# First attention of a two-layer kernel: weight tiles in all four column groups, the sums of four tiles times ones in a step of their own, denominators carried to the query side by DMA

## What is computed

```python
c_q  = h @ W_DQ + b_DQ                 # 32 wide
c_kv = h @ W_DKV + b_DKV               # 32 wide
q = concat(c_q @ W_UQ + b_UQ, c_q @ W_QR + b_QR)        # per head, 128 + 32
k = concat(c_kv @ W_UK + b_UK, h @ W_KR + b_KR)
v = c_kv @ W_UV + b_UV
attn = softmax(q @ k.T / sqrt(160))    # 2048 x 2048 for each of 8 heads
x = x + (attn @ v).reshape(s, 1024) @ W_O + b_O
...
# second attention, 16 heads of 64, 64 anchors
attn = softmax(qk @ W_anchor.T / 8)    # 2048 x 64 for each head
```

## Time and profile before

| what | us |
|---|---|
| median of 3 runs | 790.29 (788.67 to 1489.75) |
| the profiled execution's own time | 788.66 |
| span of its trace | 786.9 |
| 32 blocks of the first attention, first exponential to last | 38.6 to 525.1 |
| second attention, its 16-tile loop, about | 555 to 637 |

### The profile page before, as it was taken

The page is one execution under the profiler, slowest core; times in us unless marked ns, Lnnn a source line. Parts: engine busy times, 40 slices in busy tenths (PEclk is TensorE's granted clock), DMA queues, the critical chain, the costliest instruction groups (busy, mean ns, idle before and its releaser), DMA issues.

```text
span 786.9 us, 12800 instructions
## 1 busy us (share of the span) xinstructions
PE 761.2 (97%) x4302; PEld 473.6 (60%) x4302; DVE 584.4 (74%) x1227; ACT 453.0 (58%) x1035; POOL 569.6 (72%) x485
## 2 busy tenths in 40 slices
PE   8899999999999999999999999999799899999997
PEld 6575555555555555555555555537556589778885
DVE  7878777787777777877777777875887736875564
ACT  4266666656665665666666656564677750455543
POOL 5078999998888788788878878962679771345554
PEclk9999999999999999999999999999999999999999
DMA  6200000000000000000000000003000000000000
GB/s 159 65 3 0 1 2 1 1 2 1 1 1 1 2 1 1 1 1 0 2 1 1 1 1 1 2 1 111 0 1 1 0 2 1 1 1 13 2 14 27
DMA packets 18761, 8.46 MB, mean 11 GB/s; under 512 B 8724, under 2 KB 17957, under 8 KB 18696
## 3 DMA queue, kind: packets, MB, share of 16 engines
q1 hardware_dynamic: 17416, 7.54, 3.8%
q10 hardware_dynamic: 1280, 0.12, 0.1%
HBM read 6.53 MB, written 1.05 MB: 10 GB/s over the span
## 4 chain that ended last, share of the span: by engine, by line
PE 72%; POOL 11%; issue 9%; DVE 5%; ACT 1%; POOLq 0%; DVEq 0%
PE ps L1375 22%; PE ps L1334 17%; PE ps L1320 15%; POOL hid_lo L877 7%; PE ps L1686 4%; PE ps L1357 4%; POOL nrm L859 2%; DVE mx L925 2%; PE ps L1307 2%; POOL hid L859 1%; PE ps L1308 1%; PE ps L1382 1%; PE ps L311 1%; POOL X L865 1%; PE ps L1665 1%
## 5 line engine op out<-in xcount | busy, mean ns | idle before, releaser
L925 DVE TENSOR_REDUCE mx<-ps 128x1 f32<-128x512 f32 x512 | 320.4, 683 | 87.7 <-PE ps L1320 87.6
L527 ACT ACTIVATE prob<-ps 128x512 f32<-128x512 f32 x512 | 268.1, 605 | 135.3 <-PE ps L1334 135.3
L811 POOL TENSOR_TENSOR part<-prob 128x512 f32<-128x512 f32 x189 | 241.3, 1285 | 52.4 <-PE ps L1382 48.9
L1334 PE MATMUL ps<-q_cols,key 128*128 128x512 f32 x512 | 214.8, 422 | 0.2 <-ACT prob L527 0.2
L1320 PE MATMUL ps<-key,q_rows 128*128 128x512 f32 x512 | 202.0, 398 | 3.3 <-DVE q_rows L904 1.7
L1375 PE MATMUL ps<-prob,val 128*32 128x512 f32 x1024 | 183.5, 599 | 0.0
L1382 PE MATMUL ps<-part,ones_v 128*32 128x512 f32 x384 | 182.8, 598 | 0.0
L816 POOL TENSOR_TENSOR part<-part,prob 128x512 f32<-128x512 f32 x126 | 162.4, 1289 | 19.7 <-ACT prob L527 1.5
L1334 PEld LDWEIGHTS ps<-q_cols,key 128*128 128x128 f32 x512 | 95.6, 188 | 96.9 <-issue 75.3
L1320 PEld LDWEIGHTS ps<-key,q_rows 128*128 128x128 f32 x512 | 95.8, 188 | 29.5 <-DVE mx L925 10.7
L877 POOL TENSOR_TENSOR hid_lo<-hid,hid_hi 128x512 fp32r<-128x512 f32 x44 | 56.8, 1293 | 49.6 <-ACT hid_hi L680 49.6
(11 more groups left out here) (268 smaller groups left out, 1047.9 us busy)
## 6 DMA issues: line engine op xcount, KB each, us to landing
X<-in_L_attn_h_t_dram SPq DMA_DIRECT2D x4, 256.0 KB, 4.2
out_dram<-X SPq DMA_DIRECT2D x4, 256.0 KB, 2.3
w_raw<-in_L_ffn_w_g_dram SPq DMA_DIRECT2D x1, 704.0 KB, 4.3
w_raw<-in_L_ffn_w_u_dram SPq DMA_DIRECT2D x1, 704.0 KB, 6.0
w_raw<-in_L_ffn_w_d_dram SPq DMA_DIRECT2D x1, 704.0 KB, 7.8
w_o<-in_L_attn_W_O_dram SPq DMA_DIRECT2D x1, 512.0 KB
w_out<-in_L_attn_W_out_dram SPq DMA_DIRECT2D x1, 512.0 KB, 5.0
q_cols<-nmx SPq DMA_DIRECT2D x32, 2.0 KB, 1.9
```

Source lines behind the costliest of these rows:

```text
L527: act.activation(prob[:, g % RING, :], ps[:, g % 3, :], ACT.Exp, scale=SCALE).then_inc(s_exp, 1)
L811: pool.tensor_tensor(total, p[0], p[1], ALU.add).then_inc(s_sum, 1)
L925: dve.tensor_reduce(mx[:, n % 2, c % TPB, at:at + 1], ps[:, pair(chunk_pair(lin)) + j, :], AX.X, ALU.max).then_inc(s_mrd, 1)
L1334: pe.matmul(ps[:, g % 3, :], key[:, n // NB % KBUF, t * P:(t + 1) * P], q_cols[:, n % NB, :], start=True, stop=True).then_inc(s_sc, 1)
```

## The change

- `CHUNK_PAIR` and the second pair go: from chunk 10 on all chunks use banks 3 and 4. Bank 5 is for keys and output, bank 6 for the sums times ones, bank 7 stays. `rows_behind` now waits, in every slot, until DVE has read the same half of the chunk just before.
- `weighted` uses all four column groups for values: two batches of two steps a block (slots 6 and, for the block before, 1).
- `totals` is new (slot 2): one step of four matmuls with ones, each on a sum of four `prob` tiles.
- The sums: four of four tiles, twelve adds a block. POOL makes ten of them; DVE makes the first add of the third and the fourth sum (`begin_sum`, slots 5 and 7), and POOL waits for it. In the last block DVE makes all three adds of the fourth.
- `sums_out`: ACT copies bank 6 to `den_sb`; four DMAs on SP's queue (`denominators`) put rows 0, 32, 64, 96 of it on the query side as `den`; DVE adds the four and takes the reciprocal (`accumulate`, now in slot 6, after slot 6's chunk). `output` moves to slot 4, `keys_lo` from slot 0 to slot 1. The folded weights `proj` fill all 128 rows and lose their extra column, with three set-up memsets on POOL.
- Second attention: `prb` gets a third buffer, and the exponential of tile t waits for tile t - 3.

The core of the diff (longer removed parts are left out; they stand in the kernel above):

```diff
+        with nc.sbuf_tensor("prb2", [P, H1, A], F32) as prb2:
+            pass
...
+        NG = P // C
+        NW = NT // (2 * NG)
+        VSUM = (2, 3)
+        ADDS = NT - NG - len(VSUM)
         LEAD = CPB + 2
         KLEAD = NB
-        DW = D + 1
         U = 7
         A_BANK = (4, U)
         KB_AT = H * C1
         prob = sb("prob", [P, RING, BLK])
-        part = sb("part", [P, 2, STEPS, BLK])
+        part = sb("part", [P, 2, NG, BLK])
+        den_sb = sb("den_sb", [P, BLK])
+        den = sb("den", [P, 2, NG, TPB])
         mx = sb("mx", [P, 2, TPB, 4])
         u_sb = sb("u_sb", [P, 2, BLK])
-        rden = sb("rden", [P, 2, 2, 2])
+        dsum = sb("dsum", [P, 2, TPB])
...
-        CHUNK_PAIR = (0, 0, 1, 0, 1, 0, 0, 1)
-        def by_gpsimd(n):
-            return 1 if n == NBLK - 1 else 2
+        KEY_BANK, SUM_BANK, OUT_BANK = 5, 6, 5
+        def added(n):
+            return ADDS if n < NBLK - 1 else ADDS - 2
         def chunk_pair(lin):
-            return lin % 2 if lin < LEAD else CHUNK_PAIR[(lin - LEAD) % CPB]
+            return lin % 2 if lin < LEAD else 0
...
+                def denominators(n):
+                    sp.wait_ge(s_densb, n + 1)
+                    if n >= 2:
+                        sp.wait_ge(s_rden, 2 * (n - 1))
+                    with nc.allow_non_contiguous_dma("4 x 128 x 4 words"):
+                        for g in range(NG):
+                            sp.dma_start(den[:, n % 2, g, :], den_sb[C * g:C * g + 1, :].rearrange("a (p i) -> a p i", i=TPB)).then_inc(s_dend, 16)
                 for n in range(NBLK):
                     k = n % NB
+                    if n >= 2:
+                        denominators(n - 2)
...
+                denominators(NBLK - 2)
+                denominators(NBLK - 1)
...
+                def sums_out(n):
+                    act.wait_ge(s_ones, n + 1)
+                    if n >= 1:
+                        act.wait_ge(s_dend, 16 * NG * n)
+                    act.copy(den_sb[:, :], ps[:, SUM_BANK, :]).then_inc(s_densb, 1)
                 def exponential(n, t):
                     g = NT * n + t
                     act.wait_ge(s_sc, g + 1)
-                    if g >= RING:
-                        act.wait_ge(s_pv, NW * (n - 1) + BATCH_OF[t] + 1)
+                    if g >= RING and t == 0:
+                        act.wait_ge(s_pv, NW * (n - 1) + 1)
+                        act.wait_ge(s_sum, ADDS * (n - 1) + 6)
+                    elif g >= RING and t == NT // 2:
+                        act.wait_ge(s_pv, NW * n)
+                        act.wait_ge(s_sum, ADDS * n)
...
-                        if t == 10 and n >= 1:
+                        if t == 4 and n >= 1:
                             sums(n - 1)
+                        if t == 6 and n >= 1:
+                            sums_out(n - 1)
...
-                            act.wait_ge(s_nr, t - 1)
-                        act.activation(prb[:, t % 2], cen[:, t % 2], ACT.Exp, scale=SCALE1).then_inc(s_pr, 1)
+                        if t >= 3:
+                            act.wait_ge(s_nr, t - 2)
+                        act.activation(prb[t % 3], cen[:, t % 2], ACT.Exp, scale=SCALE1).then_inc(s_pr, 1)
...
+                def sums(n, g):
+                    total = part[:, n % 2, g, :]
+                    p = [prob[:, (NT * n + t) % RING, :] for t in range(NG * g, NG * (g + 1))]
+                    done = ADDS * n + 3 * g - sum(x < g for x in VSUM)
+                    if n >= 2 and g == 0:
+                        pool.wait_ge(s_ones, n - 1)
+                    if g in VSUM:
+                        pool.wait_ge(s_sumd, len(VSUM) * n + VSUM.index(g) + 1)
+                    else:
+                        pool.wait_ge(s_exp, NT * n + NG * g + 2)
                         pool.tensor_tensor(total, p[0], p[1], ALU.add).then_inc(s_sum, 1)
                         done += 1
-                        if len(tiles) == 3:
-                            pool.wait_ge(s_exp, NT * n + tiles[2] + 1)
-                            pool.wait_ge(s_sum, done)
...
+                    for x in (2, 3):
+                        pool.wait_ge(s_exp, NT * n + NG * g + x + 1)
+                        pool.tensor_tensor(total, total, p[x], ALU.add).then_inc(s_sum, 1)
+                        done += 1
+                        pool.wait_ge(s_sum, done)
...
+                def begin_sum(n, g):
+                    t = NT * n + NG * g
+                    total = part[:, n % 2, g, :]
+                    if n >= 2:
+                        dve.wait_ge(s_ones, n - 1)
+                    dve.wait_ge(s_exp, t + 2)
+                    dve.tensor_tensor(total, prob[:, t % RING, :], prob[:, (t + 1) % RING, :], ALU.add).then_inc(s_sumd, 1)
+                    if n == NBLK - 1 and g == NG - 1:
+                        for x in (2, 3):
+                            dve.wait_ge(s_exp, t + x + 1)
+                            dve.wait_ge(s_sumd, len(VSUM) * NBLK + x - 2)
+                            dve.tensor_tensor(total, total, prob[:, (t + x) % RING, :], ALU.add).then_inc(s_sumd, 1)
...
+                def accumulate(n):
                     k = n % NB
+                    dve.wait_ge(s_dend, 16 * NG * (n + 1))
+                    dve.tensor_reduce(dsum[:, n % 2, :], den[:, n % 2, :, :].rearrange("p g i -> p i g"), AX.X, ALU.add).then_inc(s_rden, 1)
+                    dve.wait_ge(s_rden, 2 * n + 1)
+                    dve.reciprocal(rden[:, n % 2, :], dsum[:, n % 2, :]).then_inc(s_rden, 1)
...
-                            keys_lo(n + KLEAD, pair(1))
+                        if slot == 1 and n + KLEAD < H * NB:
+                            keys_lo(n + KLEAD, KEY_BANK)
...
+                            begin_sum(n, VSUM[0])
                             if n == NBLK - 1:
                                 ln0_norm(dve, 1)
+                        if slot == 6:
                             if n >= 1:
...
+                                accumulate(n - 1)
+                            if n == NBLK - 3:
+                                ln0_stats(dve, 0)
+                            elif n == NBLK - 2:
+                                ln0_norm(dve, 0)
+                                ln0_stats(dve, 1)
+                            elif n == NBLK - 1:
                                 ln0_stats(dve, 2)
-                                last_sums(1)
-                last_sums(2)
+                        if slot == 7:
+                            begin_sum(n, VSUM[1])
...
+                def rows_behind(lin, j):
+                    before = lin - 2 if lin == LEAD else lin - 1
+                    pe.wait_ge(s_mrd, 2 * before + j + 1)
+                def output(n):
                     pe.wait_ge(s_usb, n + 1)
+                    pe.wait_ge(s_key, min(n + 1 + KLEAD + 1, H * NB))
                     for i in range(TPB):
-                        last = pe.matmul(ps[:, pair(x) + i // 2, (i % 2) * DW:(i % 2 + 1) * DW], u_sb[:, n % 2, i * P:(i + 1) * P],
-                                         proj[:, n // NB, :], start=True, stop=True)
+                        last = pe.matmul(ps[:, OUT_BANK, i * P:(i + 1) * P], u_sb[:, n % 2, i * P:(i + 1) * P], proj[:, n // NB, :],
+                                         start=True, stop=True)
                     last.then_inc(s_ops, 1)
                 def weighted(n, w):
-                    m = NW * n + w
                     if w == 0 and n >= 1:
                         pe.wait_ge(s_usb, n)
-                    if m == 0:
+                    if w == 0 and n == 0:
                         pe.wait_ge(s_val, 1)
+                    tiles = range(2 * NG * w, 2 * NG * (w + 1))
+                    pe.wait_ge(s_exp, NT * n + tiles[-1] + 1)
+                    for t in tiles:
+                        x = t % NG
+                        last = pe.matmul(ps[C * x:C * (x + 1), U, :], val[:, t, :], prob[:, (NT * n + t) % RING, :], start=(t < NG), stop=(t >= NT - NG))
+                    last.then_inc(s_pv, 1)
+                def totals(n):
+                    if n == 0:
                         pe.wait_ge(s_const, N_CONST)
...
+                        pe.wait_ge(s_cq, 4)
+                    else:
+                        pe.wait_ge(s_densb, n)
+                    pe.wait_ge(s_sum, ADDS * n + added(n))
+                    if n == NBLK - 1:
+                        pe.wait_ge(s_sumd, len(VSUM) * NBLK + 2)
+                    for g in range(NG):
+                        last = pe.matmul(ps[C * g:C * (g + 1), SUM_BANK, :], ones_v[:, :], part[:, n % 2, g, :], start=True, stop=True)
+                    last.then_inc(s_ones, 1)
...
+                        if slot == 5 and n == 0:
+                            pe.wait_ge(s_key, KLEAD + 1)
+                            pe.wait_ge(s_cq, 3)
+                            folded(1)
                         if slot == 6:
                             weighted(n, 0)
...
+                        if n >= 1:
```

(34 more changed lines are left out.)

137 lines of the change are left out of this document (37 added, 100 removed).

## The result

The changed kernel takes 834.43 us in the median, 1.057 times the time before (95% interval 1.0519 to 1.0623): slower. Forecast were 823, with 785 to 846. The profiled execution took 836.65 us, its span 834.9; the kernel before has 788.66 and 786.9.

A forecast was written before the change was run, and what follows sets the result against it. PE, busy 97%, bound the old kernel; after the change, the PE-DVE loop over one pair of banks would. Blocks +37.2, blocks 30 and 31 -1.4, end +1.5, second attention -3: +34, so 823 us, range 785 to 846.

The forecast's parts named there:

- PE waits for DVE in a loop; the block becomes longer although PE has less to do: Forecast case for the blocks: single pair of banks chains PE and DVE, 812 to 834 us, chance 0.63.
- The chain of a block, 16.06: One block followed through PE and DVE with a single pair of banks: legs sum to 16.06 us, against 15.20.
- The adds against POOL, +0.4: DVE's `begin_sum` adds in slots 5 and 7: one meets 0.4 us of a POOL add, the other nothing; bounds 0 and 2.1.
- forecast +37.2: Loss over the blocks: 29.5 blocks, each 1.26 us longer (16.46 against 15.20).
- Blocks 30 and 31 and the end of the attention, -1.4 and +1.5: Blocks without chunks gain PE's 0.90, -1.4 us; last sums through `totals`, copy and DMAs cost +1.5 (bounds -0.5 and +5).
- The DMAs are hidden: Four DMAs of denominators before `dsum` in slot 6: 3.9 us of about 6.9 available, 3.0 to spare.
- Third `prb`, -3: Second attention: the third buffer opens the loop of 4.37 a tile, PE becomes the bound; 0.22 over 14 tiles, -3 us.
- Sum: +34: Whole kernel: +37.2, -1.4, +1.5 and -3 added up, giving 823 us.
- PE stays the bound: Rival for the whole kernel: PE's gain comes through, -28.8 + 1.5 - 3, 758 us; chance 0.06.
- The holes take it: Rival for the blocks: DVE's 3 us of holes absorb its 1.4 us, 0 a block, 786 us; chance 0.14.

The follow-up runs named there:

- run 5: Changed kernel without DVE's two adds (one tile of third and fourth sum left out, constant 1 added) and with three banks for the half chunks: 769.54 us, 0.975.
- Run 4: Changed kernel with DVE's two first adds given to the first and second sum, in slots 1 and 4: 829.67 us, 1.053.
- run 7: Changed kernel with twenty more matmuls (12 and 8) where PE waits at the end of the attention: 837.03 us, 1.058.
- run 8: Changed kernel with each of the four DMAs of the denominators issued twice, once into a spare tile: 850.34 us, 1.075.
- run 3: The kernel before the change with only the third `prb` buffer of the second attention added: 785.15 us, 0.996.
- run 9: Changed kernel with three banks for half chunks, DVE beginning the first two sums in slots 1 and 3, `totals` in slot 3: 784.83 us, 0.994.
- 6: Changed kernel with three banks, DVE's adds in slot 7 and slot 1 of the next block, `totals` in slot 3: 830.39 us, 1.051.
- run 2: Changed kernel with half chunks going round three banks from block 2 on, all adds kept: 827.04 us, 1.049.
- 11: Changed kernel with three banks, DVE's adds in slots 1 and 3, `totals` in slot 3, the last block's whole fourth sum on DVE: 782.73 us, 0.987.

## Why the prediction was right, and where its sum was off

*PE waits for DVE in a loop; the block becomes longer although PE has less to do.* Right, and shown: without the adds and with three banks the block is 14.2 (run 5); with the adds and a single pair it is 16.29.

*The chain of a block, 16.06.* By its legs in the trace after:

| leg (start of the first reduction of a slot: M0) | predicted | measured |
|---|---|---|
| M0 of slot 0 to M0 of slot 2 | 0.60 + 0.79 + 2.51 + 0.44 = 4.34 | 4.38 |
| to M0 of slot 3 | 2.07 | 2.12 |
| to M0 of slot 5 | 0.60 + 0.79 + 1.36 + 0.44 = 3.19 | 3.24 |
| to `nmx` | 0.60 + 0.72 = 1.32 | 1.33 |
| to M0 of slot 0, the pile | 0.08 + 0.60 + 1.20 + 0.42 + 1.04 + 1.20 + 0.60 = 5.14 | 5.21 |
| sum | 16.06 | 16.28 |

All five are long by 0.01 to 0.07. Inside the legs two errors work against each other. The 0.79 from a reduction to the next half chunk in its bank is 0.74 to 0.75 wherever that half chunk waits (344.79 to 345.54); the matmul at 332.13 from which it was read started 0.46 behind the one before it, PE's own distance, and did not wait. PE's part of a leg is 0.05 to 0.10 longer than summed (`output` 1.46 for 1.36: 346.14 to 347.60).

*The adds against POOL, +0.4.* This term failed in the steady blocks: it is nothing there, since POOL's adds start 1.36 apart (two in 2.64) and not the 1.43 that I had from one pair in the earlier trace rows, so POOL is through 0.17 before DVE asks. It came back in five of the six early blocks, up to 1.1 an add, and in the last. 0.22 too little in the legs and 0.4 too much here gave 1.08 a block for 1.26; with the early blocks the sum to `nmx` of block 31 is +37.0, forecast +37.2. The same number for partly other reasons.

*Blocks 30 and 31 and the end of the attention, -1.4 and +1.5.* Measured +9.0: the step that failed. By three stretches, before and after: from `nmx` of block 31 to the end of the last exponential 16.99 and 18.98 (+2.0, forecast -1.4); from there to the end of the last add of `prob` tiles 1.84 and 6.93 (+5.1, in no term of the sum); from that to `pooled` 10.44 and 12.34 (+1.9, forecast +1.5). So the path that I did cost came much as forecast: DVE idles 4.53 before the last `dsum`, 2.71 before. What I had at nothing is the order of DVE's instructions, in which adds and normalization now stand in each other's way: PE waited 3.40 behind a normalization of 2.18 and an add of 1.74, and 2.99 behind one of 5.34 (4.01 at most before), and the last sum was begun 4.7 after it could have been. Which place for them would be better no run here tried.

*The router.* Not in the sum: +6.3. Before, its matmuls ran at a granted 1.00, after at 0.50 for much of it. Run 4, with another end of the attention, had it at full clock and was 5 us shorter from there. That PE's waits ahead of it bring the clock down was argued, and run 7 does not bear it out.

*The DMAs are hidden.* Right (run 8). *Third `prb`, -3.* -4.9 in the trace after (4.06 a tile in the mean, 3.98 in most, for 4.37), -4.3 alone (run 3).

Sum: +34 was forecast, +48 came. The difference of 14 lies behind `nmx` of block 31: +9 in the end of the attention, +6 in the router, -2 in the second attention. That the time still came within the range is in part its width.

*The rivals.* "PE stays the bound" needs both the adds in the pile and the single pair gone (run 5). "The holes take it" is true of the adds if they are put there: but only with a third bank, and only where POOL isn't made to wait for them (run 9 against 4 and 6).

## What to carry to other kernels

Where two engines hand a small buffer to and fro, add up one round of the loop, leg by leg: that gave the block within 0.2 us, while the busy shares said that there was room. When a third engine takes part, a relief in one loop shows only down to the next (here 16.3, then 16.0 to 16.4 through POOL, then 14.3), so single changes look worthless that are worth 2 us together. Before a change is judged by its total, look whether an instruction in the loop has become longer: in run 2 that alone hid three quarters of the gain. And price the last block by itself, in the order in which each engine must do its work there.

## What was not expected of the hardware

The same two adds cost 1.84 us a block with three banks in slots 5 and 7 (runs 2 and 5: 16.02 and 14.18), and 0.1 in slots 1 and 3 (run 9). Their own two times 0.60 are less than the 1.84, and what comes on top is the meeting with POOL, 0.8 a block in run 2. Whether they meet is a matter of phase, and the blocks settle in one and keep it: runs 9 and 11 have the same blocks, and the second add took 0.75 in one and 1.78 in the other for some 170 us, with blocks of 14.3 and 14.6.

The Trainium skill, page "SBUF — State Buffer", section "Who interferes with whom", has a VectorE instruction with two SBUF inputs contend with a GpSimd instruction that reads SBUF, under an exclusive lock. The traces agree: an add of 0.68 took up to 1.77 in the changed kernel. They also show how much the phase decides: 0.68 to 0.69 in all steady blocks of the changed kernel but one (0.85), with POOL busy for 12.85 of the 16.28 us of such a block.
